# Attention and feed-forward on one core: four instead of eight of the packed weight blocks are dequantised in the token iterations, and the token loops are written out

## The chip, the cores and the metric

One core of one Trainium2 chip runs one launch of the kernel. The metric is the device time in microseconds, the median of 3 runs: 2889.43 us (2889.09 to 2890.73).

## The reference

A batch of 64 sequences of 64 tokens with 512 channels, in float32, goes through one layer:

```python
x = x + attention(einsum('bct,bcd->bdt', x, cond_w[cond]), ...)   # each sequence is mixed over its 64 tokens
x = x + ffn(adapters(x, W, A[idx], Bm[idx], scale[idx]), gate, up, down)
# attention: q, k, v = h @ W + b; rope on q and k; 16 query heads, 8 key heads of 32;
#   routing = sigmoid(h @ Wr + br); each head keeps its 32 best of 64 keys; softmax; @ Wo + bo
# ffn: gate and up are 4096 x 512, down is 512 x 4096, each weight a 4-bit code times the
#   scale of its block of 32; out = (gelu(x @ gate.T) * (x @ up.T)) @ down.T
```

## The kernel before

All matrix products are made of three: each float32 operand is split in a high part and the rest (HI, LO), and HI*HI, HI*LO and LO*HI are summed in PSUM. The high part is a copy by ScalarE, the rest a subtraction on VectorE or GpSimd.

**Token stage.** 16 iterations of 4 sequences (256 tokens) each. Every engine has its own hand-written instruction stream, and semaphores join them; nothing reorders it. In iteration t TensorE makes the values of t, the scores of its two halves (`score`), turns the probabilities, applies them (`attend`) and makes the output projection (`out_proj`). Between these stand the head of iteration t+1 (`mixing`, `routing`, `project` for k and q) and the tail of t-1 (`adapter_ranks`, `hidden_*`, the input of the feed-forward stage). VectorE does in `iteration` (L1165): `value`, `softmax_shift` (row_max L1119, probs L1121), `softmax_sum` and `normalise` for each half, `mask_ranks` and `ranks_low` (xa_parts, L1158), `hidden`, `mixed` (hs, L1067: its second pair is what TensorE's `routing`, L638, waits for), `heads_low`, three `rope`, `top_keys`, `add_residual` (L1149), `rows_low` (L1143) and `q_low` (L1094). PSUM has only two banks for projections (`proj`), used in the fixed order `USES`.

**Dequantising.** The packed weights are 16 blocks of 256 hidden channels; a block has 6 units (gate, up, down, two nibbles each). A unit is six VectorE instructions in `dequantise` (L1033): the first half are magnitude, sign, lut_line and sign xor scale (L1045 to L1051), the second half lut_line and lut_v (L1054, L1056). GpSimd's `weight_block` (L535) waits for all six, multiplies by the signed scale (L540), splits (L548, L550) and stores the parts in `w_scratch` (L553); after the last unit of a block it waits for the stores. Each token iteration holds 3 units, k0 to k0+2, half a block; the second half of the third unit stands at the start of the next iteration, behind `value`. So blocks 0 to 7 come in the 16 iterations. GpSimd also does the rest of k and of half of q (`k_low` L562, `q_low` L567) and, first in its iteration, x+bo (L578), which waits for the store of the previous x1 and for `rows_low`, and which `add_residual` and SyncE's next x load wait for.

**Loops.** Iterations 1 to 14 are a loop of pairs, `Fori(0, NT // 2 - 1)`, on each engine (SyncE: 1 to 12 in pairs); 0 and 15 are written out. Semaphore values in a loop are computed in registers.

**Feed-forward stage.** 4 groups of 4 blocks; a group goes over 8 tiles of 512 tokens with its 4 weight slots in SBUF. A tile is 8 steps; each has 12 matmuls for gate, 12 for up and 12 for down (L624, L817). VectorE and ScalarE make gelu(gate)*up and its split, and VectorE adds the tile's result to acc (L1247). Blocks 8 to 15 are dequantised in tiles 1 to 8, one unit in each of the first six steps. Slot 0 and the first tile are loaded by SyncE before iteration 15 and in it; slot 1 after the last h_scratch store, slots 2 and 3 when also x1 and blocks 0 to 3 are stored:

```python
            for q in w_stored:
                sp.wait_ge(q, GB * 48)
            for k in range(2, GB):
                load_slot(0, k)
```

Of the kernel before, what the change touches and what calls it, by code (L numbers as in the profile page):

```python
# [44 lines left out]
def build(nc, a, out):  # L45
    B, C, D = a["x"].shape
    NCP = a["gate_packed"].shape[0]
# [3 lines left out]
    NT = B // NB  # L51
    NF = B * C // TILE
    NQ = TILE // P
    GB = 4
    NG = NCP // GB
# [15 lines left out]
    with ExitStack() as ctx:  # L71
# [214 lines left out]
        def raw_views(j):  # L286
# [3 lines left out]
            return stages[n][:, :, 0:cols], parts[:, HI], parts[:, LO]  # L290

        block = ctx.enter_context(nc.Block())


        @block.sync
        def _(sp):
# [88 lines left out]
            iteration(0, None, 0)  # L385
            with sp.Fori(0, NT // 2 - 2) as n:
                iteration(n * 2 + 1, n, 1)
                iteration(n * 2 + 2, n, 0)
            iteration(NT - 3, NF - 2, 1)
            iteration(NT - 2, NF - 2, 0, more_x=False)  # L390

# [50 lines left out]
            NPAIR = NF // 2  # L442
# [64 lines left out]
        def _(pool):  # L507
# [61 lines left out]

            def iteration(t, par, c, k0, do_head=True):  # L570


                pool.wait_ge(x1_stored, t * 16 + PRIMED)
                passed()
                pool.wait_ge(turn_used, t * NP + PRIMED)
                passed()
                for q in range(NP):
                    ins = pool.tensor_tensor(x1[:, q, :], x_in[:, par, q, :], bo[:], ALU.add)  # L578
                ins.then_inc(residual_ready, 1)
                weight_block(c, k0, False)  # L580
                if do_head:
                    k_low(t + 1)
                weight_block(c, k0 + 1, False)
                if do_head:
                    q_low(t + 1)
                weight_block(c, k0 + 2, False)

# [7 lines left out]
            load_packed(0, 1)  # L595
            load_packed(0, 2)
            iteration(0, 0, 0, 0)
            with pool.Fori(0, NT // 2 - 1) as n:
                iteration(n * 2 + 1, 1, n, 3)
                iteration(n * 2 + 2, 0, n + 1, 0)  # L600
            iteration(NT - 1, 1, NT // 2 - 1, 3, do_head=False)
            with pool.Fori(NF, NCP - 1) as c:
                for k in range(6):
                    weight_block(c, k, False)
# [7 lines left out]
        def _(pe):  # L612
# [169 lines left out]
            pe.wait_ge(raw_lo, len(RAW))  # L782
            with pe.Fori(0, NT // 2 - 1) as n:
                iteration(n * 2 + 1, 1, n + 1)
                iteration(n * 2 + 2, 0, n + 1)
            iteration(NT - 1, 1, 0, do_head=False)
# [46 lines left out]
            NPAIR = NF // 2  # L833
# [14 lines left out]
        def _(act):  # L848
# [139 lines left out]
            act.wait_ge(gather_rest, (B // 2 - 2 * NP) * 16)  # L988
            with act.Fori(0, NT // 2 - 1) as n:
                iteration(n * 2 + 1, 1)  # L990
                iteration(n * 2 + 2, 0)
            iteration(NT - 1, 1, do_head=False)
# [27 lines left out]
        def _(dve):  # L1020
# [92 lines left out]
            def value(it, q):  # L1113
                bank = full_wait(dve, it, f"v{q}")
                dve.tensor_tensor(v_sb[:, q].rearrange("p g d -> p (g d)"), bank[:, 0:256], bv[:], ALU.add).then_inc(proj_free[BANK[f"v{q}"]], 1)
# [48 lines left out]

            def iteration(t, c, k0, before, do_tail=True, do_head=True):  # L1165


                it = t
                value(it, 0)
                value(it, 1)  # L1170
                if before is not None:
                    dequantise(*before, (1,))
                softmax_shift(t, 0)
                dequantise(c, k0, (0,))
                if do_tail:
# [9 lines left out]
                if do_head:  # L1185
                    mixed(t + 1, (0, 1))
                dequantise(c, k0, (1,))
                if do_head:
# [3 lines left out]
                heads_low(t, 0)  # L1192
                dequantise(c, k0 + 1, (0,))
                if do_head:
                    rope(it, t + 1, 0)
                if do_tail:
                    hidden(t - 1, 2)
                    hidden(t - 1, 3)
                dequantise(c, k0 + 1, (1,))
                add_residual(it, t, 0)  # L1200
                if do_head:
                    top_keys(t + 1)
                heads_low(t, 1)
                dequantise(c, k0 + 2, (0,))
                if do_head:
# [23 lines left out]
            q_low(0)  # L1229
            split(7)  # L1230
            iteration(0, 0, 0, None, do_tail=False)
            with dve.Fori(0, NT // 2 - 1) as n:
                iteration(n * 2 + 1, n, 3, (n, 2))
                iteration(n * 2 + 2, n + 1, 0, (n, 5))
            iteration(NT - 1, NT // 2 - 1, 3, (NT // 2 - 1, 2), do_head=False)
            dequantise(NT // 2 - 1, 5, (1,))
            mask_ranks(BEHIND, NT - 1)
# [31 lines left out]
            NPAIR = NF // 2  # L1269

            ffn_tile(0, 0, first=True)
            ffn_tile(0, 1, block_c=NF)
            with dve.Fori(1, NPAIR) as p:
                ffn_tile(p, 0, block_c=p * 2 + NF - 1)
                ffn_tile(p, 1, block_c=p * 2 + NF)
            ffn_tile(NPAIR, 0, block_c=2 * NF - 1)
            ffn_tile(NPAIR, 1)
            with dve.Fori(NPAIR + 1, NG * NPAIR) as p:
                ffn_tile(p, 0)
                ffn_tile(p, 1)  # L1280
# [100 lines left out]
```

## Time and profile before

| | us |
|---|---|
| median of 3 runs | 2889.43 |
| lowest, highest | 2889.09, 2890.73 |
| profiled execution: its span, first to last instruction | 2885.1 |
| TensorE busy | 2746.3 (95%) |
| VectorE busy | 1596.2 (55%) |
| ScalarE busy | 807.1 (28%) |
| GpSimd busy | 586.5 (20%) |
| granted TensorE clock, mean | 0.991 |

No time of its own is given for the profiled execution beside its span; the median of the runs lies 4.3 us above that span. Iteration 0 begins at 50 us, iteration 1 at 99 us, iteration 15 at 740 us and the first feed-forward tile at 789 us. The chain that ended last is 83% TensorE and 10% VectorE. "issue" names idle time for which the profile shows no releaser. Matmul busy times of neighbours overlap, since their ends are modelled; their starts are exact. SPq is SyncE's DMA queue.

### The profile page before, as it was taken

The page shows a single profiled execution, that of the slowest core. Times are in us where ns is not written, and L with a number is a line of the kernel's source. Part 1 is how long each engine was busy: PE and PEld are TensorE (multiplying, and loading weights), DVE is VectorE, ACT ScalarE, POOL GpSimd, SP SyncE. Part 2 cuts the span into 40 slices and gives each one's busy share as a digit, 9 for nine tenths or more (in the row PEclk, how much of TensorE's full clock was granted, in tenths as well). Part 3 has the DMA queues.
Part 4 walks back from the last instruction along what each step waited for, and adds up shares of the span by engine and source line. Part 5 has one row for each costly group of instructions (what it writes and reads, how often), then busy time and mean ns, then how long its engine had stood idle before and what let it go on. Part 6 is the DMA issues. An engine that isn't in the chain of part 4 may idle for free.

```text
span 2885.1 us, 40412 instructions
## 1 busy us (share of the span) xinstructions
PE 2746.3 (95%) x14592; PEld 2300.8 (80%) x14592; DVE 1596.2 (55%) x2668; ACT 807.1 (28%) x1369; POOL 586.5 (20%) x613
## 2 busy tenths in 40 slices
PE   5888888898799999999999999999999999999999
PEld 4777777777688888888888888888888888888887
DVE  5888988889646666666333333333333333333333
ACT  3444434344222222222222222222222222222221
POOL 7444434444404444443000000000000000000000
PEclk8999999999999999999999999999999999999999
DMA  4222322222553343346211121611121153111110
GB/s 132 92 103 90 104 95 104 96 104 89 198 211 132 146 146 137 131 173 242 74 72 58 64 81 56 235 58 58 58 87 58 58 202 118 58 58 58 58 58 29
DMA packets 102583, 301.64 MB, mean 105 GB/s; under 512 B 16360, under 2 KB 34664, under 8 KB 96368
## 3 DMA queue, kind: packets, MB, share of 16 engines
q1 hardware_dynamic: 76400, 224.25, 21.5%
q0 software_dynamic: 26112, 76.60, 7.3%
q8 instruction: 24, 0.39, 0.1%
q14 instruction: 47, 0.39, 0.0%
HBM read 191.34 MB, written 109.45 MB: 104 GB/s over the span
## 4 chain that ended last, share of the span: by engine, by line
PE 83%; DVE 10%; issue 5%; ACT 1%; DVEq 0%; SPq 0%; another core or an unknown queue 0%; DMA 0%; ACTq 0%
PE gate L624 24%; PE up L624 24%; PE down L817 24%; PE proj L624 9%; DVE row_max L1119 1%; DVE row_sum L1126 1%; DVE hs L1067 1%; DVE rope_sin L1084 1%; DVE magnitude L1045 1%; DVE rope_sin L1087 1%; DVE lut_line L1054 1%; PE pv L689 1%; DVE rope_in L1089 0%; DVE h_out L1162 0%; DVE xa_parts L1158 0%
## 5 line engine op out<-in xcount | busy, mean ns | idle before, releaser
L624 PE MATMUL gate<-h_in,w_slot 128*128 128x512 f32 x3072 | 739.6, 390 | 2.8 <-issue 2.8
L624 PE MATMUL up<-h_in,w_slot 128*128 128x512 f32 x3072 | 737.9, 389 | 0.0
L817 PE MATMUL down<-w_slot,inter_parts 128*128 128x512 f32 x3072 | 737.5, 389 | 0.0
L624 PEld LDWEIGHTS gate<-h_in,w_slot 128*128 128x128 f32 x3072 | 577.7, 188 | 123.0 <-issue 3.0
L624 PEld LDWEIGHTS up<-h_in,w_slot 128*128 128x128 f32 x3072 | 576.6, 188 | 119.8
L817 PEld LDWEIGHTS down<-w_slot,inter_parts 128*128 128x128 f32 x3072 | 576.6, 188 | 119.7
L1267 DVE TENSOR_TENSOR inter_parts<-inter,inter_parts 128x512 fp32r<-128x512 f32 x256 | 180.3, 704 | 538.3 <-ACT inter_parts L1012 538.3
L1256 DVE SCALAR_TENSOR_TENSOR gate_in<-gate_sq,gate 128x512 f32<-128x512 f32 x256 | 176.0, 687 | 466.8 <-ACT gate_sq L1002 466.8
L1012 ACT ACTIVATE inter_parts<-inter 128x512 fp32r<-128x512 f32 x256 | 161.8, 632 | 923.7 <-PE down L817 711.8
L1002 ACT ACTIVATE gate_sq<-gate 128x512 f32<-128x512 f32 x256 | 153.0, 598 | 492.9 <-PE gate L624 492.9
L1262 DVE SCALAR_TENSOR_TENSOR gate_val<-gate_tanh,gate 128x512 f32<-128x512 f32 x256 | 175.5, 686 | 129.3 <-ACT gate_tanh L1004 129.3
L540 POOL TENSOR_TENSOR lut_v<-lut_v,signed_scale 128x512 f32<-128x512 f32 x96 | 123.1, 1282 | 512.8 <-DVE lut_v L1056 512.8
L1004 ACT ACTIVATE gate_tanh<-gate_in 128x512 f32<-128x512 f32 x256 | 161.9, 632 | 194.0 <-DVE gate_in L1256 194.0
L1265 DVE SCALAR_TENSOR_TENSOR inter<-gate_val,up 128x512 f32<-128x512 f32 x256 | 176.1, 688 | 24.8
L550 POOL TENSOR_TENSOR w_parts<-lut_v,w_parts 128x512 fp32r<-128x512 f32 x96 | 145.9, 1520 | 7.9
L624 PE MATMUL proj<-x1T,w 128*128 128x256 f32 x768 | 103.5, 285 | 21.5 <-DVE xa L1153 20.5
L624 PEld LDWEIGHTS proj<-x1T,w 128*128 128x128 f32 x768 | 94.7, 191 | 24.7 <-DVE xa L1153 23.5
L624 PE MATMUL proj<-hs,wq 128*128 128x256 f32 x768 | 96.2, 285 | 6.1 <-ACT rope_in L875 6.1
L624 PEld LDWEIGHTS proj<-hs,wq 128*128 128x128 f32 x768 | 92.7, 191 | 9.4 <-issue 6.8
L624 PE MATMUL proj<-wo,attnT 128*128 128x512 f32 x384 | 96.8, 400 | 2.8 <-DVE h_out L1162 1.9
L624 PEld LDWEIGHTS proj<-wo,attnT 128*128 128x128 f32 x384 | 69.7, 188 | 18.9 <-DVE h_out L1162 3.2
L1247 DVE TENSOR_TENSOR acc<-down,acc 128x512 f32<-128x512 f32 x128 | 79.5, 682 | 2.1 <-PE down L817 2.1
(105 smaller groups left out, 2271.1 us busy)
## 6 DMA issues: line engine op xcount, KB each, us to landing
h_in<-h_scratch SPq DMA_DIRECT2D x32, 2048.0 KB, 7.9
w_scratch<-w_parts POOLq DMA_DIRECT2D x96, 512.0 KB, 3.0
w_slot<-w_scratch SPq DMA_DIRECT2D x16, 3072.0 KB, 11.1
acc<-out SPq DMA_DIRECT2D x32, 1024.0 KB, 5.4
out<-acc SPq DMA_DIRECT2D x32, 1024.0 KB, 4.4
h_scratch<-h_out SPq DMA_DIRECT2D x64, 256.0 KB, 2.6
x_in<-in_x SPq DMA_DIRECT2D x16, 512.0 KB, 3.8
out<-x SPq DMA_DIRECT2D x16, 512.0 KB, 2.8
```

Of the source, the lines that this page charges most:

```text
L540: pool.tensor_tensor(lut_v[:, par, :], lut_v[:, par, :], signed_scale[:, par, :].bitcast(F32), ALU.mult).then_inc(w_used, 1)
L550: pool.tensor_tensor(w_parts[:, par, LO, :], lut_v[:, par, :], w_parts[:, par, HI, :].bitcast(F32), ALU.subtract).then_inc(w_step, 1)
L624: ins = pe.matmul(out_ap, lhsT, rhs, start=(start and n == 0), stop=(stop and n == len(pairs) - 1))
L817: ins = pe.matmul(down[tc][:], inter_parts[:, j % 2, u, tc * P:(tc + 1) * P], w_slot[k][:, 2, nib_n, v, :], start=(j == 0 and m == 0), sto ...
L1002: act.activation(gate_sq[:], gate[b][:], ACT.Square).then_inc(sq_done, 1)
L1004: act.activation(gate_tanh[:], gate_in[:], ACT.Tanh, scale=GELU_SCALE * GELU_CUBIC).then_inc(tanh_done, 1)
L1012: act.activation(inter_parts[:, b, HI, :], inter[:], ACT.Copy).then_inc(inter_hi, 1)
L1247: dve.tensor_tensor(acc[par][:, tc, :], down[tc][:], acc[par][:, tc, :], ALU.add).then_inc(acc_added, 1)
L1256: dve.scalar_tensor_tensor(gate_in[:], gate_sq[:], 1.0 / GELU_CUBIC, gate[b][:], ALU.add, ALU.mult).then_inc(gin_done, 1)
L1262: dve.scalar_tensor_tensor(gate_val[:], gate_tanh[:], 1.0, gate[b][:], ALU.add, ALU.mult).then_inc(gval_done, 1)
L1265: dve.scalar_tensor_tensor(inter[:], gate_val[:], 0.5, up[b][:], ALU.mult, ALU.mult).then_inc(inter_done, 1)
L1267: dve.tensor_tensor(inter_parts[:, b, LO, :], inter[:], inter_parts[:, b, HI, :].bitcast(F32), ALU.subtract).then_inc(inter_ready, 1)
```

## The change

A table gives iteration t one unit if t is even and two if it is odd, 24 units in all, that is blocks 0 to 3. No unit crosses from one iteration into the next any more: of the (at most) two units of an iteration, `first` has the places of k0 and `second` those of k0+1, and the place of k0+2 is gone. Blocks 4 to 15 are dequantised in feed-forward tiles 1 to 12. All token loops are written out in Python, so iterations 1 to 14 are straight-line code with constant semaphore values on all five engines.

```diff
+        EARLY = GB
+        SLOTS = [1 if t % 2 == 0 else 2 for t in range(NT)]
+        UNITS = [[divmod(u, 6) for u in range(sum(SLOTS[:t]), sum(SLOTS[:t + 1]))] for t in range(NT)]
+        assert sum(SLOTS) == 6 * EARLY
...
@@ sync
-            with sp.Fori(0, NT // 2 - 2) as n:
-                iteration(n * 2 + 1, n, 1)
-                iteration(n * 2 + 2, n, 0)
-            iteration(NT - 3, NF - 2, 1)
-            iteration(NT - 2, NF - 2, 0, more_x=False)
+            for t in range(1, NT - 1):
+                iteration(t, (t - 1) // 2, t % 2, more_x=t < NT - 2)
@@ gpsimd
                 ins.then_inc(residual_ready, 1)
-                weight_block(c, k0, False)
+                weight_block(*UNITS[t][0], False)
                 if do_head:
                     k_low(t + 1)
-                weight_block(c, k0 + 1, False)
+                if len(UNITS[t]) > 1:
+                    weight_block(*UNITS[t][1], False)
                 if do_head:
                     q_low(t + 1)
-                weight_block(c, k0 + 2, False)
...
-            iteration(0, 0, 0, 0)
-            with pool.Fori(0, NT // 2 - 1) as n:
-                iteration(n * 2 + 1, 1, n, 3)
-                iteration(n * 2 + 2, 0, n + 1, 0)
-            iteration(NT - 1, 1, NT // 2 - 1, 3, do_head=False)
-            with pool.Fori(NF, NCP - 1) as c:
+            for t in range(NT):
+                iteration(t, t % 2, do_head=t < NT - 1)
+            with pool.Fori(EARLY, NCP - 1) as c:
@@ tensor
-            with pe.Fori(0, NT // 2 - 1) as n:
-                iteration(n * 2 + 1, 1, n + 1)
-                iteration(n * 2 + 2, 0, n + 1)
+            for t in range(1, NT - 1):
+                iteration(t, t % 2, (t + 1) // 2)
@@ vector
-            def iteration(t, c, k0, before, do_tail=True, do_head=True):
+            def iteration(t, do_tail=True, do_head=True):
                 it = t
+                first, second = UNITS[t][0], (UNITS[t] + [None])[1]
                 value(it, 0)
                 value(it, 1)
-                if before is not None:
-                    dequantise(*before, (1,))
                 softmax_shift(t, 0)
-                dequantise(c, k0, (0,))
+                dequantise(*first, (0,))
...
-                dequantise(c, k0, (1,))
+                dequantise(*first, (1,))
...
-                dequantise(c, k0 + 1, (0,))
+                if second is not None:
+                    dequantise(*second, (0,))
...
-                dequantise(c, k0 + 1, (1,))
+                if second is not None:
+                    dequantise(*second, (1,))
...
                 heads_low(t, 1)
-                dequantise(c, k0 + 2, (0,))
...
-            ffn_tile(0, 1, block_c=NF)
-            with dve.Fori(1, NPAIR) as p:
-                ffn_tile(p, 0, block_c=p * 2 + NF - 1)
-                ffn_tile(p, 1, block_c=p * 2 + NF)
-            ffn_tile(NPAIR, 0, block_c=2 * NF - 1)
-            ffn_tile(NPAIR, 1)
+            ffn_tile(0, 1, block_c=EARLY)
+            LATE = (NCP - EARLY) // 2
+            with dve.Fori(1, LATE) as p:
+                ffn_tile(p, 0, block_c=p * 2 + EARLY - 1)
+                ffn_tile(p, 1, block_c=p * 2 + EARLY)
+            ffn_tile(LATE, 0, block_c=NCP - 1)
+            ffn_tile(LATE, 1)
```

ScalarE's token loop is written out in the same way as TensorE's. Two places show what moved. The first is VectorE at the end of iteration 0 and the start of iteration 1, before (the first rows of the loop; ISA and REGISTER_ALU rows compute semaphore values):

```order
L1143 TENSOR_TENSOR x1T<-turn,x1T 128x4x128
L1232 UNCONDITIONAL_BRANCH
L1232 ISA
L1115 TENSOR_TENSOR v_sb<-proj,bv 128x256
L268 REGISTER_ALU
L1115 TENSOR_TENSOR v_sb<-proj,bv 128x256
L1053 ISA
L1054 SCALAR_TENSOR_TENSOR lut_line<-magnitude,lut_line 128x512
L1055 REGISTER_ALU
L1056 SCALAR_TENSOR_TENSOR lut_v<-magnitude,lut_line 128x512
L1118 ISA
L1119 TENSOR_REDUCE row_max<-scores 128x16
```

and the same place now:

```order
L1140 TENSOR_TENSOR x1T<-turn,x1T 128x4x128
L1112 TENSOR_TENSOR v_sb<-proj,bv 128x256 x2
L1116 TENSOR_REDUCE row_max<-scores 128x16
L1118 TENSOR_TENSOR probs<-scores,row_max 128x2x8x64
L1042 TENSOR_SCALAR magnitude<-packed 128x512
```

The branch, the register work and the second half of the third unit are gone from between `value` and row_max. The second place is GpSimd at the same point, from its store of an iteration's second unit to x+bo of the next iteration, before:

```order
L553 DMA w_scratch<-w_parts 128x1024
L567 TENSOR_TENSOR q_parts<-rope_in,q_parts 128x2x4x64
L540 TENSOR_TENSOR lut_v<-lut_v,signed_scale 128x512
L548 CAST w_parts<-lut_v 128x512
L550 TENSOR_TENSOR w_parts<-lut_v,w_parts 128x512
L553 DMA w_scratch<-w_parts 128x1024
L598 UNCONDITIONAL_BRANCH
L598 ISA
L575 ISA
L578 TENSOR_TENSOR x<-x_in,bo 128x512 x2
```

and now (iteration 0 has one unit, so its store is the first unit's):

```order
L555 DMA w_scratch<-w_parts 128x1024
L564 TENSOR_TENSOR rope_in<-rope_in,k_whole 128x512
L569 TENSOR_TENSOR q_parts<-rope_in,q_parts 128x2x4x64
L580 TENSOR_TENSOR x<-x_in,bo 128x512 x2
```

x+bo follows `q_low` directly; the third unit, which waited for VectorE's second half in the next iteration, no longer stands between them.

## Rows read from the trace of the kernel before

**Rows 1.** The page's 40 slices, busy tenths of TensorE.
```profile
PE   5888888898799999999999999999999999999999
```

**Rows 2.** Stretches: us, busy us (instructions) of each engine, PEclk, DMA share, GB/s.
```profile
98.89:740.29 641.40, 560.67 (x4706) 488.18 (x4704) 573.57 (x1065) 280.26 (x516) 275.13 (x280) 0.99 0.28 99
...
853.90:1400.00 546.10, 546.10 (x2411) 452.16 (x2411) 354.36 (x592) 123.43 (x201) 227.59 (x248) 1.00 0.42 156
...
1400.00:1950.00 550.00, 550.00 (x2428) 455.44 (x2427) 204.99 (x303) 125.95 (x203) 0.00 (x0) 1.00 0.24 86
```

**Rows 3.** VectorE in order of time, iterations 5 and 6; its wait for "issue".
```profile
283.24 0.76 DVE L1115 TENSOR_TENSOR v_sb<-proj,bv 128x256 f32<-128x256 f32 x2 [2.33 <-issue]
...
283.91 0.68 DVE L1054 SCALAR_TENSOR_TENSOR lut_line<-magnitude,lut_line 128x512 f32<-128x512 int32 x1
...
285.24 1.22 DVE L1119 TENSOR_REDUCE row_max<-scores 128x16 f32<-128x1024 f32 x1
...
322.83 0.69 DVE L1149 TENSOR_TENSOR x<-proj,x 128x512 f32<-128x512 f32 x1 [0.31 <-PE proj L624]
...
330.13 1.22 DVE L1119 TENSOR_REDUCE row_max<-scores 128x16 f32<-128x1024 f32 x1
...
DVE v_sb L1115 <- issue: 13.4, 6, 2.3
```

**Rows 4.** TensorE in order of time, iterations 4 to 6.
```profile
281.07 1.68 PE L664 MATMUL scores<-k_diagonal,q_parts 128*128 128x256 f32 x12
...
300.34 1.57 PE L624 MATMUL proj<-hs,wr 128*16 128x256 f32 x12 [1.14 <-DVE hs L1067]
...
319.74 3.05 PE L624 MATMUL proj<-wo,attnT 128*128 128x512 f32 x12
...
328.39 1.65 PE L664 MATMUL scores<-k_diagonal,q_parts 128*128 128x256 f32 x12
...
344.95 2.67 PE L624 MATMUL proj<-hs,wr 128*16 128x256 f32 x12 [1.15 <-DVE hs L1067]
```

**Rows 5.** VectorE in order of time, what stretch A and a quiet unit take.
```profile
287.63 1.49 DVE L1045 TENSOR_SCALAR magnitude<-packed 128x512 int32<-128x512 int32 x1
...
292.05 1.12 DVE L1158 TENSOR_TENSOR xa_parts<-xa,xa_parts 128x256 fp32r<-128x256 f32 x1
...
300.11 1.21 DVE L1126 TENSOR_REDUCE row_sum<-probs 128x16 f32<-128x1024 f32 x1
...
317.52 0.41 DVE L1045 TENSOR_SCALAR magnitude<-packed 128x512 int32<-128x512 int32 x1
...
319.13 0.01 DVE L1084 LOAD_MASK_SELECT rope_sin<-rope_in  x1
...
333.66 1.50 DVE L1049 TENSOR_SCALAR lut_line<-magnitude 128x512 f32<-128x512 int32 x1
...
337.43 0.36 DVE L1158 TENSOR_TENSOR xa_parts<-xa,xa_parts 128x256 fp32r<-128x256 f32 x1
...
344.72 1.21 DVE L1126 TENSOR_REDUCE row_sum<-probs 128x16 f32<-128x1024 f32 x1
```

**Rows 6.** GpSimd and SyncE's queue in order of time, and the page's DMA issues.
```profile
287.54 1.30 POOL L550 TENSOR_TENSOR w_parts<-lut_v,w_parts 128x512 fp32r<-128x512 f32 x1
...
290.38 2.50 POOL L578 TENSOR_TENSOR x<-x_in,bo 128x512 f32<-128x512 f32 x2 [0.15 <-issue]
...
339.00 2.50 POOL L578 TENSOR_TENSOR x<-x_in,bo 128x512 f32<-128x512 f32 x2 [2.79 <-DMA w_scratch<-w_parts]
...
323.78 0.39 SPq L373 DMA_DIRECT2D out<-x  x1
...
out<-x SPq DMA_DIRECT2D x16, 512.0 KB, 2.8
```

**Rows 7.** GpSimd and SyncE's queue, end of iteration 15.
```profile
770.72 0.60 POOL L553 DMA_DIRECT2D w_scratch<-w_parts  x1 [0.64 <-POOL w_parts L550]
...
789.24 3.36 SPq L376 DMA_DIRECT2D w_slot<-w_scratch  x3
```

More of the change, by code:

```diff
@@ L568, in q_low, with iteration @@
                                    q_parts[:, HI, 0].rearrange("p b r c -> p r b c").bitcast(F32), ALU.subtract).then_inc(q_ready[0], 1)
-            def iteration(t, par, c, k0, do_head=True):
+            def iteration(t, par, do_head=True):
                 pool.wait_ge(x1_stored, t * 16 + PRIMED)
@@ L988, in _ @@
             act.wait_ge(gather_rest, (B // 2 - 2 * NP) * 16)
-            with act.Fori(0, NT // 2 - 1) as n:
-                iteration(n * 2 + 1, 1)
-                iteration(n * 2 + 2, 0)
+            for t in range(1, NT - 1):
+                iteration(t, t % 2)
             iteration(NT - 1, 1, do_head=False)
@@ L1230, in _ @@
             split(7)
[L1231 to L1236, printed above, removed]
+            iteration(0, do_tail=False)
+            for t in range(1, NT - 1):
+                iteration(t)
+            iteration(NT - 1, do_head=False)
             mask_ranks(BEHIND, NT - 1)
@@ L1271, in _ @@
             ffn_tile(0, 0, first=True)
-            ffn_tile(0, 1, block_c=NF)
-            with dve.Fori(1, NPAIR) as p:
-                ffn_tile(p, 0, block_c=p * 2 + NF - 1)
-                ffn_tile(p, 1, block_c=p * 2 + NF)
-            ffn_tile(NPAIR, 0, block_c=2 * NF - 1)
-            ffn_tile(NPAIR, 1)
-            with dve.Fori(NPAIR + 1, NG * NPAIR) as p:
+            ffn_tile(0, 1, block_c=EARLY)
[5 more added lines that the diff above has]
+            ffn_tile(LATE, 1)
+            with dve.Fori(LATE + 1, NG * NPAIR) as p:
                 ffn_tile(p, 0)
```

## The prediction

> **What bounds the kernel now.** I read the slices first [rows 1]: TensorE is at nine tenths or more from the eleventh slice on and mostly at eight before, in the token stage. So the two stages have different limits. The stretches give sizes [rows 2]. Iterations 1 to 14 take 641.40 us, with VectorE busy 573.57 and TensorE 560.67: neither bounds them alone. In the feed-forward tiles TensorE is never idle: 2411 matmuls in 546.10 us while blocks are dequantised, 2428 in 550.00 us with none, 4.415 per us in both. Dequantising costs nothing there.
>
> So the token iteration has to be read as a chain. In iterations 5 and 6 it goes as follows.
> - A, VectorE alone: from the first row_max to the second pair of `mixed`, which ends where row_sum starts. 285.24 to 300.11 and 330.13 to 344.72 [rows 3, 5]: 14.87 and 14.59 us. TensorE's routing waits for its end and starts 0.2 us later.
> - B, TensorE alone: from routing to the end of the second output projection, 300.34 to 322.79 [rows 4], 22.45 us. VectorE does its second and third unit beside this and still waits 0.31 us for the projection before the residual add at 322.83 [rows 3].
> - C: residual, last rope, the q split, then TensorE's first scores, which end at 328.39+1.65=330.04 [rows 4]; 7.2 us. In iteration 6 row_max follows at 330.13 [rows 3], so there the chain is tight.
> - Only after the branch of the token loop it isn't: the scores are ready at 281.07+1.68=282.75 [rows 4], but row_max starts at 285.24 [rows 3].
>
> A unit that VectorE sheds in B is therefore worth nothing; what counts is what it sheds in A and behind the branch.
>
> **The change part by part.** The profiled execution has a span of 2885.1 us; the median of the runs is 4.3 us longer, and I keep that distance for the new kernel.
>
> 1. *The branch, and the third unit's second half.* In the iterations that follow a loop branch (3, 5, ... 13: six) VectorE idles 2.2 us before `value` (13.4 us in six times), and then does lut_line and lut_v of the unit before, 283.91 to 285.24, 1.33 us [rows 3]. Both go. What is late next are the scores, at 282.75. The gain is 285.24-282.75=2.49 us, six times: **14.9 us**. In the other iterations the 1.33 us lie under TensorE's scores (330.04 against 330.13): nothing. The bounds are 0, if another wait takes the place, and 6x(2.2+1.33)=21 us, if the scores came earlier as well.
> 2. *GpSimd beside VectorE in A.* Some VectorE instructions of A take far longer than in a quiet place. In iteration 5 magnitude takes 1.49 us against 0.41 (at 317.52), and the xa_parts split 1.12 against 0.36 [rows 5]: 1.84 us in all. GpSimd runs its split of the third unit at 287.54 and x+bo at 290.38 beside them [rows 6]. Without that A is 14.87-1.84=13.03 us. In iteration 6 it is 14.59, 1.56 us over this, most of it in one instruction of 1.50 us at 333.66 where 0.4 is usual [rows 5], again beside the third unit's work on GpSimd. The change takes this unit away. x+bo then waits only for rows_low, which ends shortly before `value` at 328.1, and for the store of x1, issued at 323.78 and landed 2.8 us later [rows 6]. So its two adds, 2.50 us, run from some 328.3 to 330.8, while A's first 0.4 us instruction comes at 332.5; in between VectorE runs value, row_max and probs<-scores. Odd iterations follow the first pattern, 1 to 15, even ones the second, 2 to 14: 8x1.84+7x1.56=**25.6 us**. The bounds: all of it, or, if the adds come later and hold one short instruction by 1.08 us as at 287.63, 15x1.08=16.2 us less. I take all of it, since 1.7 us lie between.
>    The Trainium skill (GPSIMD Engine Reference, section Key points) says that GpSimd shares its SBUF interfaces with VectorE and collides with instructions in a 2-port mode or with two SBUF inputs. The trace bears this out for the 0.4 us instructions. By that page the add is free beside value, row_max and probs<-scores, which have at most one SBUF input; were it to come later, normalise with its two inputs would be held too, which no row here shows. That is rival R1.
> 3. *The other units.* 24 of 48 units leave the token stage. In a quiet place a unit takes VectorE 319.13-317.52=1.61 for its first half [rows 5] and 1.33 us for its second [rows 3], 2.94 us. Those in B are hidden by TensorE's 22.45 us: 0. Iteration 0 sheds two units in the same places: 0.
> 4. *Iteration 15 and the first tile.* Block 3 now ends in iteration 15, at the place of today's second unit, whose store is issued at 770.72 [rows 7]. Slots 1 to 3 are loaded from 789.24 on [rows 7], since h_scratch and x1 are stored first; 18 us remain: 0.
> 5. *Twelve blocks in tiles 1 to 12:* 0 by the rate above. Group 1 needs blocks 4 to 7 at tile 8, and they are done in tiles 1 to 4. If the cover failed, four more tiles would pay 6x2.94=17.6 us each, but tiles 1 to 8 do just this work today.
> 6. *Clock.* The granted clock is 0.99 over the loop [rows 2]. In iteration 6 routing takes 2.67 us against 1.57 in iteration 5 [rows 4], 1.1 us, part of it at the lower of the two levels (1.2 and 2.4 GHz) after stretch A, in which TensorE often waits. I leave this as it is: 0. Its ends are 0.01x641=6 us of gain, if it never falls, and 14x1.1=15 us of loss, if it falls in every iteration.
>
> Sum: 14.9+25.6=40.5 us off. Time 2889.4-40.5=**2848.9 us**, rounded 2849; span 2844.6. About 0.2% (6 us) is what a measurement of this kernel can tell from no change.
>
> **Rivals.**
> - *R1, the collision only moves.* x+bo, or GpSimd's first unit, which is still there, falls on other short instructions of A. For: in iteration 6 x+bo waits 2.79 us for a DMA [rows 6]. Against: that DMA is w_scratch's at the end of a block, and the end of a block moves into B. Gain 40.5-16.2=24: 2865 us.
> - *R2, VectorE is the bound after all.* Every unit counts in full: 24x2.94=71 us, and 13.4 for the branches: 2805 us. Against: the wait at 322.83, and B's length.
> - *R3, the clock.* VectorE sheds work in just the stretch in which TensorE waits, so the falls may go: 6 us more gain, 2843 us. The Trainium skill (TensorE: Matmul & The Clock Gate, section HAM oscillation) ties the fall of the clock to idle gaps between matmuls, which speaks for this side; the trace has the fall behind A, as it says.
> - *R4, slower: straight-line code does not arrive fast enough.* A loop replays one body; written out, 14 iterations of 4706/14=336 matmuls and as many weight loads [rows 2] have to be brought in one after the other. A stall like the one at the branch, 2.2 us, in an engine's own part of the chain costs 14x2.2=31 us at one per iteration, which leaves a gain of 10. From 1.3 per iteration on the kernel is slower; at two it is 2889.4-40.5+61.6=2911 us. Against: iterations 0 and 15 and tile 1 are straight-line today, VectorE's only wait for "issue" at `value` is the branch's [rows 3], and tile 1 lies in a stretch without any gap [rows 2].
>    The Trainium skill (Runtime: NRT & Kernel Launch, section Instruction fetch mechanics) says that instructions are prefetched in sequence and that a taken branch out of the window waits for a fetch; by that page the branch's wait goes and R4 has almost no chance.
> - *R5, next to nothing:* another wait takes the place of both terms, as the bias rows or GpSimd's q split, which now stands behind a block's last store. 2884 to 2890 us.
>
> **How the numbers follow.** Forecast (35 to 47 us off, R3 included): 0.76. R1: 0.14. R2: 0.03. R5: 0.03. R4: 0.04. Predicted is the likeliest, 2849. The range holds the forecast with its clock term and reaches through R1: 2841 to 2866. It leaves out R2, R4 and R5, 0.10, and about as much again for sizes that I may have wrong. Faster by over 0.2%: 0.95; within: 0.02; slower: 0.03, since part of R4 and R5 lands on a smaller gain.
>
> **What would show it.** Right: from one `value` to the next 42.9 us (1.9 to row_max, 13.0 for A, 0.2, 22.45 for B, 5.3 to `value`) in nearly all of iterations 1 to 14; no idle time before `value`; magnitude at 0.41 us behind the first probs<-scores; x+bo before it; routing still waiting for `mixed`; the tiles at 4.415 matmuls per us. Wrong: a new idle time in B, waits for "issue" in the iterations, magnitude still at 1.5, or TensorE idle in tiles 9 to 12.

## The result, and the profile after

The changed kernel takes 2838.36 us (median of 4 runs, 2836.91 to 2841.54); the kernel before takes 2889.26 us beside it (2887.54 to 2890.73). The ratio is 0.9827, with a 95% interval of 0.9813 to 0.9841. It is faster, as forecast, but by 51 us instead of 40.5: the time lies 2.6 us below the low end of the range (2841 us). Measured again on another chip, it came out at 0.9827 once more (experiment 8 below).

The page of the changed kernel has these lines; the first is its span, the third answers to [rows 1].

```profile
span 2836.1 us, 38641 instructions
...
PE 2729.4 (96%) x14592; PEld 2292.2 (81%) x14592; DVE 1565.1 (55%) x2668; ACT 806.1 (28%) x1369; POOL 589.1 (21%) x613
...
PE   4899999999899999999999999999999999999999
```

TensorE's row is at nine tenths in the token stage now too. The stretches say the same in microseconds (columns as in [rows 2]: us, then busy us of PE, PEld, DVE, ACT, POOL, the granted clock, DMA share, GB/s). The first stretch is iterations 1 to 14, the second is iteration 15 up to the first gate matmul, the third lies in the tiles with dequantising, the last in those without.

```profile
99.68:695.98 596.30, 546.93 (x4706) 481.56 (x4704) 478.28 (x939) 279.77 (x516) 175.55 (x170) 1.00 0.23 80
695.98:740.92 44.94, 34.67 (x285) 29.90 (x283) 26.20 (x43) 10.24 (x18) 12.44 (x12) 0.92 0.50 189
809.50:1355.00 545.50, 545.50 (x2408) 451.84 (x2407) 362.67 (x608) 123.89 (x201) 244.41 (x271) 1.00 0.44 161
1905.00:2455.00 550.00, 550.00 (x2428) 455.58 (x2427) 205.09 (x304) 126.00 (x203) 0.00 (x0) 1.00 0.24 88
```

Iterations 1 to 14 fell from 641.40 to 596.30 us, 45.1 us less. The same stretch of iteration 15 took 48.49 us before and takes 44.94, 3.55 less. The rest, up to the end, went from 2885.1-788.78=2096.3 to 2836.1-740.92=2095.2 us. Iteration 0 is 1.0 us longer, and started 0.25 us earlier. Together 49.0 us of span. The tiles run at 2408/545.50=4.414 and 2428/550.00=4.415 matmuls per us: four more blocks there cost nothing.

VectorE in order of time, iteration 5 (answers to [rows 3, 5]):

```profile
269.92 0.75 DVE L1112 TENSOR_TENSOR v_sb<-proj,bv 128x256 f32<-128x256 f32 x2
271.90 1.23 DVE L1116 TENSOR_REDUCE row_max<-scores 128x16 f32<-128x1024 f32 x1 [1.23 <-PE scores L663]
...
274.30 0.42 DVE L1042 TENSOR_SCALAR magnitude<-packed 128x512 int32<-128x512 int32 x1
...
277.65 0.36 DVE L1155 TENSOR_TENSOR xa_parts<-xa,xa_parts 128x256 fp32r<-128x256 f32 x1
...
284.88 1.21 DVE L1123 TENSOR_REDUCE row_sum<-probs 128x16 f32<-128x1024 f32 x1
...
307.61 0.69 DVE L1146 TENSOR_TENSOR x<-proj,x 128x512 f32<-128x512 f32 x1 [1.48 <-PE proj L623]
...
312.92 0.75 DVE L1112 TENSOR_TENSOR v_sb<-proj,bv 128x256 f32<-128x256 f32 x2
```

No idle time stands before `value`. row_max waits for the scores of TensorE. magnitude takes 0.42 us and xa_parts 0.36, where it was 1.49 and 1.12. Stretch A is 284.88-271.90=12.98 us (forecast: 13.03). The residual waits 1.48 us for the projection: in B VectorE has room. From value to value it is 43.00 us, as in iterations 1, 9 and 13; the other ten take 42.4 to 42.5 (iterations are counted from the first `value` of each).

GpSimd's x+bo now stands where the prediction put it, right after `rows_low` and before A's first short instruction at 274.30 (answers to [rows 6]):

```profile
270.18 2.53 POOL L580 TENSOR_TENSOR x<-x_in,bo 128x512 f32<-128x512 f32 x2 [5.89 <-DVE x1T L1140]
```

The clearest picture is TensorE's waits over the whole stretch. First the kernel before, 98.9 to 740 us (us in total, times, longest):

```profile
PE proj L624 <- DVE xa L1153: 19.8, 14, 1.8
PE proj L624 <- DVE hs L1067: 16.2, 14, 1.3
PE turn L697 <- DVE x L1149: 11.0, 14, 0.8
PE scores L659 <- DVE q_parts L1094: 10.2, 14, 0.8
PE proj L624 <- DVE v_sb L1115: 5.8, 6, 1.1
```

and the changed one, 99 to 696 us:

```profile
PE proj L623 <- DVE hs L1064: 14.9, 14, 1.1
PE scores L658 <- DVE q_parts L1091: 11.5, 15, 0.8
PE turn L696 <- DVE x L1146: 11.0, 14, 0.8
```

The waits for xa (in A) and for v_sb (behind the branch) are gone, and so is one for xa_parts (4.2 us in six times before); the others have changed by 1.3 us or less. In A's first half, from the first scores to the turn of the probabilities, TensorE now works nearly without a gap:

```profile
270.18 1.68 PE L663 MATMUL scores<-k_diagonal,q_parts 128*128 128x256 f32 x12
271.70 1.54 PE L623 MATMUL proj<-x1T,wa 128*128 128x256 f32 x12
...
275.18 2.99 PE L623 MATMUL proj<-x1T,w 128*128 128x256 f32 x24
278.07 0.97 PE L623 MATMUL proj<-xa_parts,wb 128*128 128x256 f32 x6
279.20 1.09 PE L672 MATMUL scores<-identity,probs 128*128 128x128 f32 x8 [0.16 <-DVE probs L1130]
```

Before, the xa wait stood between these. The prediction took A for "VectorE alone"; in the changed kernel it no longer is, and experiment 6 shows what that means.

### The profile page after: what moved, and what is told of

It is laid out like the page before. It is cut to its first block, busy times and chain, and to the rows that moved or that the text cites. A ratio compares the mean times of both kernels' runs of the same rounds, so it can differ in the third digit from the quotient of the medians.

```text
span 2836.1 us, 38641 instructions
## 1 busy us (share of the span) xinstructions
PE 2729.4 (96%) x14592; PEld 2292.2 (81%) x14592; DVE 1565.1 (55%) x2668; ACT 806.1 (28%) x1369; POOL 589.1 (21%) x613
## 4 chain that ended last, share of the span: by engine, by line
PE 86%; DVE 10%; issue 2%; ACT 1%; SPq 0%; DMA 0%; another core or an unknown queue 0%; DVEq 0%; ACTq 0%
PE gate L623 25%; PE up L623 25%; PE down L815 24%; PE proj L623 10%; DVE row_max L1116 1%; PE scores L663 1%; DVE row_sum L1123 1%; DVE probs L1118 1%; PE pv L688 1%; DVE hs L1064 1%; DVE probs L1130 1%; DVE rope_sin L1081 1%; DVE rope_in L1086 1%; DVE rope_in L1083 1%; DVE rope_sin L1084 0%
## 5 line engine op out<-in xcount | busy, mean ns | idle before, releaser
L623 PEld LDWEIGHTS proj<-wo,attnT 128*128 128x128 f32 x384 | 69.7, 188 | 17.6 <-DVE h_out L1159 1.9
```

The costliest lines, as they stand in the source:

```text
L623: ins = pe.matmul(out_ap, lhsT, rhs, start=(start and n == 0), stop=(stop and n == len(pairs) - 1))
```

## The experiments

Each ratio is against runs of the kernel before on the same chip: experiments 1 to 4 shared one chip (before: 2887.2 us), 5 to 7 another (2885.3), 8 to 10 a third (2884.4). The theory comes from the prediction: time is saved behind the branch (term 1) and where GpSimd's work falls on VectorE's short instructions in A (term 2), and units in B are free. Since the gain was 51 us and not 40.5, the question is also what it left out.

**1. The loops alone.** The kernel before, all token loops written out, all 48 units where they were:

```diff
-            with dve.Fori(0, NT // 2 - 1) as n:
+            for n in range(NT // 2 - 1):
                 iteration(n * 2 + 1, n, 3, (n, 2))
                 iteration(n * 2 + 2, n + 1, 0, (n, 5))
```

and the same on the other four engines.

> The kernel before with its token loops written out on all five engines, and all 48 units where they were. Theory (the branch and the third unit are two separate terms): value no longer waits 2.2 us in six iterations, row_max starts 2.24 us earlier there, the collisions in A stay: 13.4 us off, 2876 us, with the clock falls of before (granted clock 0.991). Rival (the 10 us by which I was short come from the straight-line code itself, on any engine): some 24 us off, 2865 us.

Measured: 2867.10 us, ratio 0.9930 (0.9913 to 0.9946). These 20.1 us lie between the theory's 13.4 and the rival's 24, and nearer to the rival. From value to value the even iterations, which ended with the idle time of the branch, take 44.0 to 44.2 us instead of some 46.4, and the odd ones 44.7 to 44.8 instead of 44.9: 2.5 us per pair, 15 us in six, of which some 14 are the branch's idle time (six times 2.3 to 2.4) and 1 is 0.15 us in each odd iteration. Iterations 1 to 14 take 621.93 us, 19.5 less. The collision is still there: VectorE's magnitude in iteration 5 beside GpSimd's split of the third unit, first VectorE, then GpSimd.

```profile
281.87 1.22 DVE L1114 TENSOR_REDUCE row_max<-scores 128x16 f32<-128x1024 f32 x1
283.12 1.22 DVE L1116 TENSOR_TENSOR probs<-scores,row_max 128x1024 f32<-128x1024 f32 x1
284.26 1.50 DVE L1040 TENSOR_SCALAR magnitude<-packed 128x512 int32<-128x512 int32 x1
```

```profile
284.18 1.29 POOL L547 TENSOR_TENSOR w_parts<-lut_v,w_parts 128x512 fp32r<-128x512 f32 x1
286.10 0.60 POOL L550 DMA_DIRECT2D w_scratch<-w_parts  x1 [0.63 <-POOL w_parts L547]
286.72 2.69 POOL L575 TENSOR_TENSOR x<-x_in,bo 128x512 f32<-128x512 f32 x2
```

That leaves 19.5-15=4.5 us for a second thing, which the prediction had at zero: TensorE's falls to the lower clock. In the profiled execution before, four iterations (2, 6, 11 and 13, granted clock 0.96) are longer than their neighbours by 1.6, 1.5, 0.6 and 0.6 us, 4.3 us together; here none is. No unit was shed in this experiment, so the falls went with the loops. How the loops do it isn't shown; TensorE's wait for v_sb is gone and that for xa is 13.1 us instead of 19.8.

A third thing stands at the end of iteration 15, at the first gate matmuls of the feed-forward stage: the kernel before, this experiment, and the changed kernel.

```profile
788.78 4.58 PE L624 MATMUL gate<-h_in,w_slot 128*128 128x512 f32 x12 [2.78 <-issue]
```

```profile
770.49 3.01 PE L621 MATMUL gate<-h_in,w_slot 128*128 128x512 f32 x12 [0.98 <-issue]
```

```profile
740.92 3.01 PE L623 MATMUL gate<-h_in,w_slot 128*128 128x512 f32 x12 [0.98 <-issue]
```

The wait before them is 1.8 us shorter and they run at the higher clock sooner, here as in the changed kernel. With TensorE's loop rolled the wait is 2.60 us (experiment 2) and 1.64 us (experiment 7); in all others it is 0.98. So this gain too comes with the loops and not with the units.

**2. VectorE's loop alone.** Only VectorE's loop written out, the others rolled.

> The kernel before with the loop written out on VectorE alone. Theory: the branch costs only where the engine waits in its chain, and that is VectorE: the same time as e1_loops_only within 2 us, 2876. Rival (TensorE, ScalarE, GpSimd or SyncE pay for their branches and register work too): a part of the gain is missing, 2880 to 2886.

Measured: 2870.43 us, 0.9942 (0.9925 to 0.9958). That is 3.3 us over experiment 1, a little more than the 2 us of the theory and below the rival's 2880. The iterations are nearly as in experiment 1 (44.9 and 44.1 us) but for one fall of the clock (45.64 us in iteration 6). So the branch that costs in the iterations is VectorE's; the loops of the other engines are worth some 3 us together, the one fall included.

**3. The third unit at home.** Experiment 1, with the second half of the third unit no longer behind `value` of the next iteration but behind `rows_low` of its own; all 48 units stay in the token stage.

```diff
                 rows_low(t, 0)
+                dequantise(c, k0 + 2, (1,))
...
-                if before is not None:
-                    dequantise(*before, (1,))
```

> All loops written out, all 48 units still in the token stage, but the third unit's second half stands behind rows_low in its own iteration, so that GpSimd does this unit in B and x+bo right behind rows_low. Theory (the place of the work counts, not its amount): A falls to 13.0 us, B grows by up to 1 us where VectorE has no slack left: 2841 to 2853 us, within 15 us of the changed kernel. Rival (VectorE's load is what the change removed, 24 units of 2.94 us): no better than e1_loops_only, 2876 us.

Measured: 2900.53 us, 1.0046 (1.0029 to 1.0063): slower than the kernel before, and outside both expectations. In the iteration shown A did fall, to 301.91-288.95=12.96 us, as term 2 says; in the next one x+bo waited for a store and fell on magnitude again (1.47 us, A=14.02). But the added 1.3 us stand ahead of the residual in B, which had 0.3 us of room [rows 3], and lut_v, beside GpSimd's split of q (324.47 to 326.03), takes 0.94 us more than elsewhere, in every iteration. VectorE at the end of B:

```profile
324.23 0.68 DVE L1049 SCALAR_TENSOR_TENSOR lut_line<-magnitude,lut_line 128x512 f32<-128x512 int32 x1
324.94 1.63 DVE L1051 SCALAR_TENSOR_TENSOR lut_v<-magnitude,lut_line 128x512 f32<-128x512 int32 x1
326.50 0.68 DVE L1144 TENSOR_TENSOR x<-proj,x 128x512 f32<-128x512 f32 x1
...
328.50 1.10 DVE L1082 TENSOR_TENSOR rope_sin<-rope_sin,sin 128x512 f32<-128x512 f32 x1
```

and TensorE, which waits for that residual, and then has a value projection of 4.41 us where 3.12 is usual:

```profile
327.24 0.99 PE L694 MATMUL turn<-identity,x 128*128 128x128 f32 x4 [2.63 <-DVE x L1144]
327.87 4.41 PE L621 MATMUL proj<-wv,hs 128*128 128x256 f32 x24
```

Over iterations 1 to 14 the wait of the turn for the residual is

```profile
PE turn L694 <- DVE x L1144: 39.4, 14, 3.0
```

against 11.0 us in both kernels above: 28 us, or 2.0 per iteration (1.33+0.94-0.3=1.97), and a granted clock of 0.97 in this stretch where it is 0.99 or 1.00 in the others. Two things follow. A unit in B is free only up to B's slack, and an overrun is paid in full; the clock falls come on top, since the value projection behind the wait takes over 4 us in nearly every iteration. And the third unit can't simply be put in order at this place; the table of units in the change takes it out of the token stage. Whether another place in B would hold it wasn't tried.

**4. x+bo later.** The changed kernel, with GpSimd's x+bo held until VectorE has read the first scores. No other line changes.

```diff
                 passed()
+                pool.wait_ge(scores_used, t * NP + 1)
+                passed()
                 for q in range(NP):
```

> The changed kernel, but GpSimd's x+bo waits in each iteration until VectorE has done the first probs<-scores, so that it falls on the first half of the unit and on xa_parts. It measures the collision by itself. Theory: magnitude or a neighbour takes 1.5 us instead of 0.4 and A is 1.1 to 1.8 us longer, 15 times: 2855 to 2866 us; and if the length of A is what lets the clock fall, the granted clock goes back from 0.995 towards 0.991, some 4 us more. Rival (the collision is hidden by TensorE's own work in A): 2838 to 2842 us.

Measured: 2873.82 us, 0.9951 (0.9935 to 0.9968). The adds start 4.6 us behind `value` (283.05 against 278.44) instead of 0.3, and that takes back some 36 of the 51 us (0.9827 of this chip's 2887.2 would be 2837). GpSimd, then VectorE:

```profile
283.05 2.72 POOL L582 TENSOR_TENSOR x<-x_in,bo 128x512 f32<-128x512 f32 x2 [10.24 <-DVE probs L1120]
```

```profile
280.39 1.22 DVE L1118 TENSOR_REDUCE row_max<-scores 128x16 f32<-128x1024 f32 x1 [1.20 <-PE scores L665]
281.65 1.22 DVE L1120 TENSOR_TENSOR probs<-scores,row_max 128x1024 f32<-128x1024 f32 x1
282.79 0.42 DVE L1044 TENSOR_SCALAR magnitude<-packed 128x512 int32<-128x512 int32 x1
283.12 1.51 DVE L1045 TENSOR_SCALAR signed_scale<-packed 128x512 int32<-128x512 int32 x1
284.55 1.50 DVE L1048 TENSOR_SCALAR lut_line<-magnitude 128x512 f32<-128x512 int32 x1
...
295.54 1.21 DVE L1125 TENSOR_REDUCE row_sum<-probs 128x16 f32<-128x1024 f32 x1
```

A pair of adds holds two short instructions, by 1.09 us each. A is 295.54-280.39=15.15 us instead of 12.98: 2.17 us, 30.4 in fourteen iterations. The stretch is 629.22-596.30=32.9 us longer; the other 3 are the clock, which falls again in iterations 5 and 11 (46.15 us each, neighbours 44.6). So the place of one pair of adds of 2.5 us is worth more than the whole of term 2, which was the adds on xa_parts and GpSimd's split on magnitude. Rival R1 would have been worse than its price of 1.08 us per iteration.

The Trainium skill (GPSIMD Engine Reference, section Key points) names two kinds of VectorE instruction that collide with GpSimd: those in a 2-port mode and those with two SBUF inputs. Which mode the 0.4 us instructions above run in, no row shows; the trace shows only that they are held. Of the second kind the kernel before had xa_parts, 1.12 us instead of 0.36 [rows 5], and experiment 3 has lut_v, 1.63 us instead of 0.69, and rope_sin, 1.10 instead of 0.69, all beside GpSimd's work. There the trace agrees with the page. In the changed kernel x+bo lies beside `value` and row_max, and these stay at 0.75 and 1.23 us.

**5. Five blocks instead of four.** Six more units in the token stage, all in B.

```diff
-        EARLY = GB
-        SLOTS = [1 if t % 2 == 0 else 2 for t in range(NT)]
+        EARLY = GB + 1
+        SLOTS = [1 if t in (0, NT - 2) else 2 for t in range(NT)]
```

> The changed kernel with a fifth block in the token iterations: 30 instead of 24 units, two per iteration in all but iterations 0 and 14; the feed-forward tiles 1 to 11 do the other eleven. The six added units stand in stretch B. Theory (units in B are free as long as VectorE's work there ends before the second output projection): VectorE now idles about 2.0 us before the residual in iterations with one unit and little in those with two, so a second unit of 2.94 us can cost up to 0.9 us each at most: within 3 us of the changed kernel in the same call, 2838 to 2842 us. Rival (what counts is VectorE's load in the token stage, wherever it stands): 6 x 2.94 = 17.6 us more, 2856. If instead the last store of block 4 delays the first tile, the loss is in iteration 15 and the values before stay at 42.4 to 43.0 us.

Measured: 2838.35 us, 0.9835 (0.9819 to 0.9852), within the noise of the changed kernel's 0.9827. The rival (17.6 us more) is out. The iterations tell a little more: 42.94 to 43.10 us in all but iteration 14, which still has one unit and takes 42.46, against 42.4 in most of the changed kernel; iterations 1 to 14 take 601.33 us, 5 more. The cause can be read at the first output projection, which waits for VectorE's h_out:

```profile
PE proj L623 <- DVE h_out L1159: 3.1, 13, 0.3
```

In the changed kernel this wait comes 4 times (iterations 1, 5, 9, 13), and those are its iterations of 43.0 us. There VectorE's sign instruction of the second unit takes 1.51 us (288.48 in iteration 5) beside GpSimd's split at 288.18. In iterations 3, 7 and 11 GpSimd has no scales and codes to fetch between its product and its split, the split comes earlier (201.64 in iteration 3), the collision is shorter (magnitude takes 0.92 us, sign 0.42), and the wait isn't there. So a second unit in B costs 0.5 us at most, by a collision, not by its own 2.94 us.

**6. The first half of the first unit one iteration early,** from A to the end of B of the iteration before.

```diff
                 softmax_shift(t, 0)
-                dequantise(*first, (0,))
...
                 heads_low(t, 1)
+                if t < NT - 1:
+                    dequantise(*UNITS[t + 1][0], (0,))
```

> The changed kernel with the first half of each iteration's first unit (1.61 us of VectorE: magnitude, sign, lut_line, xor) moved out of stretch A, to the end of stretch B of the iteration before. Theory A (stretch A is VectorE's alone, as the prediction had it, and the move takes its first half's work out of the chain): A falls from 12.98 to 11.4 us, 15 x 1.6 = 24 us off, 2814. Theory B (TensorE runs without a gap through the first half of stretch A, turns and scores of its own, so that is a bound of its own, and the moved 1.61 us fill B's idle 2.0 us in single-unit iterations but overrun it by over 1 us in those with two): A keeps over 12 us, B grows in odd iterations, 2835 to 2850. A's length and the wait before the residual tell them apart.

Measured: 2836.95 us, 0.9838 (0.9822 to 0.9855). A lost 1.61 us of work and got 0.2 us shorter. VectorE, iteration 3: it now waits for ScalarE instead.

```profile
181.26 1.23 DVE L1116 TENSOR_REDUCE row_max<-scores 128x16 f32<-128x1024 f32 x1 [1.20 <-PE scores L663]
182.52 1.22 DVE L1118 TENSOR_TENSOR probs<-scores,row_max 128x1024 f32<-128x1024 f32 x1
183.66 0.41 DVE L1150 TENSOR_TENSOR xa<-proj,adapter_mask 128x256 f32<-128x256 f32 x1
184.87 1.22 DVE L1123 TENSOR_REDUCE row_sum<-probs 128x16 f32<-128x1024 f32 x1 [0.80 <-ACT probs L897]
...
188.31 0.77 DVE L1159 TENSOR_TENSOR h_out<-proj,h_out 128x256 fp32r<-128x256 f32 x2 [0.53 <-ACT h_out L918]
...
194.04 1.21 DVE L1123 TENSOR_REDUCE row_sum<-probs 128x16 f32<-128x1024 f32 x1
```

A is 194.04-181.26=12.78 us, against 12.98. So in the changed kernel A's first half is bound by VectorE and by TensorE with ScalarE at once. Theory A is out; of theory B the number 12 us and the total hold, but not its overrun in B: iterations 2 to 4 take 42.3 us. The clock fell in iterations 1, 5 and 11 (43.8 us each), though A is at its shortest here.

**7. Only VectorE and GpSimd written out.** The changed kernel, with the loops of TensorE, ScalarE and SyncE rolled as before.

> The changed kernel with TensorE's, ScalarE's and SyncE's token loops rolled again; VectorE and GpSimd, whose order the change needs, stay written out. Theory: only VectorE's branch costs time, so iterations 1 to 14 stay within 1 us of the changed kernel's 596.3; in iteration 15 ScalarE's h_out waits for the h_scratch stores again, 1 to 3 us: 2839 to 2843 us in all. Rival (written-out code of the other engines brings part of the gain, by their own branches or fewer falls of the clock): 5 us or more over the changed kernel, spread over iterations 3, 5, ... 13, 2844 or more.

Measured: 2839.45 us, 0.9842 (0.9826 to 0.9859). Iterations 1 to 14 take 599.65 us, 3.4 more, which is between the theory (under 1) and the rival (5 or more): 1.5 are one fall of the clock (iteration 10, 44.09 us), the rest 0.1 us per iteration. Against the changed kernel's ratio the whole is some 4 us longer, less than the 6 us that the measurement can tell. The wait of ScalarE's last h_out for h_scratch came back (2.8 us at the longest), and first looked like an effect of SyncE's loop; but it is there in experiment 9 (3.4 us) and not in experiment 1, which are the same kernel. So it varies from run to run, and what decides it stays open.

**8 to 10. The changed kernel, experiment 1 and experiment 6 again,** together on one chip, 5 runs each.

> The changed kernel itself, on the same chip as the next two. Theory: the part of its gain that this text did not foresee lies in the clock (falls in iterations 2, 6, 11, 13 of the profiled execution of before, 4.3 us, none in the changed one) and in iteration 15. So it should repeat within 0.2% of 0.983 of before, and the chip's draw of iterations 0 and 15 may move its span by 2 to 3 us either way. If the first measurement was a lucky one instead, the ratio comes out at 0.986 or above, which is the 2849 us of the forecast.

> The kernel before with all token loops written out, once more, beside the changed kernel. From the first time (0.9930): the loops bring 20 us, of which the branch 6 x 2.35 = 14 and the rest clock and tail; the changed kernel must then lie 25 to 30 us below this one (15 x 1.7 = 25.6 of collisions and little else). If the units shed in stretch B counted at all, the distance would be over 35.

> The first half of each first unit one iteration early, beside the changed kernel, to see whether it beats it. In its first profile even iterations were 0.15 us shorter (stretch A now waits for ScalarE and TensorE) and three iterations had a fall of the clock of 1.5 us. Theory: same within 3 us. Beating it would take 6 us or more.

| | us | ratio | iterations 1 to 14 | iteration 15 to the first gate matmul |
|---|---|---|---|---|
| before | 2884.37 | 1 | | |
| 9: loops only | 2860.13 | 0.9918 (0.9905 to 0.9932) | 621.14 | 48.37 |
| 8: changed | 2833.03 | 0.9827 (0.9813 to 0.9840) | 596.15 | 44.57 |
| 10: first half early | 2835.31 | 0.9831 (0.9817 to 0.9844) | 597.52 | 47.02 |

The changed kernel repeats its ratio. It lies 27.1 us below the loops alone, inside the 25 to 30 us expected of collisions and little else, so the 24 units shed count only for where they stood. Experiment 9 again has no fall of the clock; experiment 10 again has three (iterations 3, 9 and 13). Moving yet more out of A brings nothing: experiment 6 doesn't beat the changed kernel, and none of these versions does.

## Why the prediction was right and wrong

- **Term 1, the branch: right.** Forecast 14.9 us; experiment 1 has about 14 in the six iterations, 15 with the 0.15 us of the odd ones, and experiment 2 pins it on VectorE. The third unit's second half was worth next to nothing by itself: in experiment 1 it still stands there, and row_max starts 2.0 us behind `value` as in the changed kernel.
- **Term 2, the collision in A: right.** Forecast 25.6 us, 23.8 of them in iterations 1 to 14. There experiment 1 and the changed kernel differ by 621.93-596.30=25.6 us, of which 1.5 are B (below), so 24.1; iteration 15 brings its 1.7 us (A 13.36 us before, 11.65 now). A is 12.98 us instead of 13.03. x+bo lies where the prediction put it. The sign that the prediction named, 42.9 us from value to value, holds only in iterations 1, 5, 9 and 13; its own terms give 43.1 us for odd and 42.4 for even iterations, and the even ones do take 42.4.
- **Term 3, units in B at nothing: right, with a footnote.** The 0.31 us before the residual became 1.48 us of slack and more, and experiment 5 put six units back for nothing measurable. But "in B" is not a licence: experiment 3 put 1.3 us more of work per iteration there and paid 28 us. What the prediction missed is a small gain: in iterations 3, 7 and 11 the fewer fetches of GpSimd shorten a collision in B, 3 x 0.5=1.5 us.
- **Term 4, iteration 15 and the first tile at nothing: too small.** 3.55 us off where term 2 had 1.84 for it, and 1.1 us more in the first tile. The 1.7 us over are the wait before the first gate matmuls, 2.78 us before and 0.98 now; the 1.1 us are the first gate group, which ran partly at the lower clock before (4.58 us, granted clock 0.61) and doesn't now (3.01 us). Experiment 1 has both with all 48 units in place, so they came with the loops. This part varies: the changed kernel had 44.94 and 44.57 us in iteration 15, its near copies of experiments 5 and 6 47.0 and 47.1, by the clock in the last adapter matmuls (2.90 instead of 1.62 us for the first twelve).
- **Term 5, tiles at nothing: right**, 4.415 per us.
- **Term 6, the clock at nothing: this is the step that failed.** It was a term of the sum, put at 0 although its own bound was 6 us of gain, and it measured 4.3 us, the largest miss. The routing after the wait in A ran at the lower clock in iterations 2 and 6 before (2.55 and 2.67 us, [rows 4]); the granted clock from 344.95 to 346.50 us was 0.53. In iterations 11 and 13 A itself is longer, 15.5 us instead of 14.9; the clock from 567 to 576 us, in iteration 11, was 0.82. In the changed kernel routing takes 1.54 to 1.57 us in all of iterations 1 to 14. R3 named this gain, but its reason, the work that VectorE sheds, isn't borne out: experiments 1 and 9 shed nothing, have A at 14.5 to 14.7 us and no fall either. Experiments 3 and 4, with longer waits, have falls; but so have 6 and 10, with the shortest A. What lets the clock fall in this kernel stays open. That the falls went with the loops rests on two profiled executions without a fall (experiments 1 and 9) against one with four.
   The Trainium skill (TensorE: Matmul & The Clock Gate, section HAM oscillation) has gaps between matmuls let the clock fall. Experiments 3 and 4 agree with that, and experiments 6 and 10 show that the length of A alone doesn't tell when.
- **The distance from span to median: also failed.** I carried 4.3 us over. In the runs since, a run's time is 1.3 to 1.9 us over its own span; the profiled execution before was by that some 2.7 us faster than the median, and the changed kernel's is 0.9 us below its own. That gives 2.0 us more.

In numbers: 40.5 forecast; +4.3 clock, +1.5 in B, +0.6 of small differences in iterations 1 to 14, +1.7 iteration 15, +1.1 first tile, -0.8 iteration 0, +2.0 distance to the median: 50.9. The clock alone would have left the time in the range (2844.6 us); every miss but one has the same sign, and together they end outside it. Of these, 7.1 us (clock, iteration 15, first tile) are things that writing out the loops brought beside VectorE's branch: the prediction counted only that branch. Iteration 0 and the distance to the median are scatter: from `value` to `value` iteration 0 took 49.7 us in the changed kernel and 45.0 in its repeat, experiment 8. R2 (2805 us), R4 (instructions too slow) and R5 are out by the time. VectorE waits for "issue" nowhere in the iterations any more; TensorE's weight loads show such waits as before, none over 1.0 us.

## What to carry to other kernels

Where stages are chains of two engines, cut an iteration at the places at which one waits for the other, and price an edit by the stretch that it lands in: here 1.3 us of VectorE's work per iteration, placed at the end of one stretch, made TensorE wait 28 us more, and a whole unit of 2.94 us cost nothing or 0.5 us elsewhere in the same stretch. Look for the same VectorE instruction at two lengths (here 0.4 and 1.5 us): here it was GpSimd's work on top of it, and moving the neighbour by 4 us can be worth more than removing work. Test the parts of a change one by one: here writing out the loops brought 20 us, where its one priced term was 15. And when several side terms (clock, tail, distance from a profiled execution to the median) all point one way, put their middle in the sum instead of zero, and widen the range on that side.

## What the runs showed of the hardware

- GpSimd's two adds of [128, 512] float32 (2.5 to 2.7 us) hold VectorE's 0.41 us instructions at 1.5 us, two of them per pair (experiment 4). Beside GpSimd's work VectorE's instructions with two SBUF inputs take longer too: xa_parts 1.12 us instead of 0.36 beside the adds, lut_v 1.63 instead of 0.69 beside the split of q (experiment 3). GpSimd itself is lengthened too: its split took 2.29 us instead of 1.28 in iteration 3 of the changed kernel.
- A taken branch of the token loop cost VectorE 2.2 to 2.3 us each time, while the rolled loops of TensorE, ScalarE and SyncE together cost 0.13 us per iteration (experiment 7).
- A lower mean clock goes with the longer runs. Nine runs of the kernel before on one chip span 2879.9 us (mean clock 0.995) to 2886.8 us (0.988), and the three slowest are those at 0.988; five of experiment 9 there lie within 3.1 us.
- Straight-line code of 14 iterations brought no new wait for "issue" there; VectorE's, 13.4 us, is gone.
